# Relu attention on one core: query chunks written out, first score operands computed in place, VectorE takes the second late bank

## Chip, cores and metric

One core of a Trainium2 chip. The metric is device time in microseconds (us) of one execution, all inputs starting in HBM and the output ending there. Before the change it was measured three times: 451.36, 455.20 and 450.78 us, median 451.36 us.

## The reference

x is [2048, 128] in float32. The attention has 16 heads of width 8, and relu in place of softmax.

```python
x = L0_attn_x
h = layernorm(x)
q, k, v = split((h @ w_qkv).reshape(S, 16, 24), 3)     # 16 heads, 8 wide
w = relu(q @ k.T / sqrt(8))                            # 2048 x 2048 per head
w = w / (sum(w, -1) + 1e-6)
y = h + (w @ v) @ w_out + b_out
x = x + layernorm(y) * gamma + beta
h = layernorm(x)
real = h @ cos(theta + theta_noise)
imag = h @ sin(phi + phi_noise)
out = x + sqrt(real * real + imag * imag)
```

## The kernel before

The engines' programs are written out by hand with semaphores; nothing is scheduled by a tool. The 2048 queries are cut into four chunks of 512. A **pass** is one chunk `c`: for each of four head groups `g` (four heads each) it goes over the 16 key tiles `k` (128 keys each), so a pass has 64 **steps**, numbered `s = 16 g + k`.

A step on TensorE is `score_step` (four matmuls of 32 rows by 512 columns, one per head, the K operand with its high and low float32r parts and the Q operand with its parts side by side in 32 rows, L854) and, two steps behind (`LAG = 2`), `value_step` (the four heads' relu results times V, L884, collected in a `pv` bank over the 16 key tiles; a column of ones in V gives the sum). Scores go to three pairs of PSUM banks, `sc[0]` to `sc[2]`. Each step uses two pairs, the **early** pair (heads 0, 1) and the **late** pair (heads 2, 3). A pair is used again three pairs later, so the late half of a step waits until both relus of the early pair of the step before have been taken.

ScalarE and VectorE apply the relu and move the scores to SBUF (`w_buf`, four steps deep). ScalarE takes the first bank of the early and of the late pair (L464, L467). VectorE takes the second bank of the early pair (L602) and of the late pair (L606). At the steps in `BOTH_LATE_ACT` ScalarE takes both banks of the late pair in one activation of 1024 columns, and VectorE takes only the early one: seven, five, four and four steps of the four groups, 20 of 64 in every pass.

```python
BOTH_LATE_ACT = ((3, 8, 9, 10, 11, 13, 14), (1, 3, 8, 12, 15), (3, 7, 11, 15), (3, 7, 11, 15))
```

Beside the relus, VectorE has other work at fixed steps: `normalise` at step 3 of each group (L615 to L619), the low parts of K and Q (`low_part`, L580), in pass 0 the range reduction of the FFN angles (`trig_angles`, L630 to L646, steps 9 to 15 of group 1 and step 0 of group 2), and from pass 1 on the residual and layernorms of the chunk before (`after_pass`, L656 to L690).

Pass 0 is written out. Passes 1 to 3 are one hardware loop on each engine (`with pe.Fori(1, NC) as c`, the same on ScalarE and VectorE; SyncE and GpSimd have a shorter one), in which the semaphore values to wait for are computed in registers. The last line of the loop on TensorE is the score and value work of step 63; the next instruction after the branch is the score of step 0.

**The start.** The first 512 rows of x are loaded in one DMA (L303), normalised (`statistics`, L560 to L566; `normalise_x`, L572), transposed on TensorE (L773), copied by ScalarE (L434) and multiplied by the K and Q weights (L785, L791). ScalarE writes the high float32r part (L438, L442), VectorE the low part (L580), and then DMAs spread them over the partitions of `k_rep` and `q_rep` (row `4 r + j` holds row `r` of the high or low part), because a score matmul wants the four products high and low side by side. The first score waits for `q_lo_ready`, six dummy matmuls (`warm_up`, L809) and the DMAs. On GpSimd the three copies of the weights (L350) come when they have landed, then the padding of V for group 0 (`pad_v`, memsets L354, L355), then the normalisation of the chunks 1 to 3 (L363, L366).

Into the first ten steps of pass 0 are put the transposes and projections of the chunks 2 and 3, at hooks like `((0, 3), lambda: project_k(2))`, which stand after the score of the next step.

## Time and profile before

| what | value |
|---|---|
| median of three runs | 451.36 us |
| the profiled execution | 452.41 us |
| its span, first to last instruction | 450.6 us |
| mean granted TensorE clock in it | 0.986 |
| score starts in the span (L854) | 19.0 us to 431.5 us |
| TensorE busy | 431.3 us, 96% |
| VectorE busy | 335.6 us, 74% |
| ScalarE busy | 342.2 us, 76% |

The profiled execution took 1.8 us more than its span, and 1.05 us more than the median of the runs. In the rows, PE is TensorE's matmul and PEld its weight load, DVE is VectorE, ACT ScalarE, POOL GpSimd and SPq the DMA queue of SyncE. A timeline row has the start in us, the time in us, the engine, the line, the operation and its operands, and how many were merged; in brackets stands the idle time ahead of it with what ended it. Rows of L854 and L884 are the four score or value matmuls of one step (fp32 matmuls count as two). "issue" is time in which the engine waited for nothing that the profile shows. A step is measured from one L854 row to the next.

### The profile page before, as it was taken

To read this page: it belongs to the slowest core of one execution; us is meant where nothing else is said; L and a number is where in the kernel's file an instruction comes from. 1 tells how busy PE (TensorE), PEld (TensorE's weight loads), DVE (VectorE), ACT (ScalarE), POOL (GpSimd) and SP (SyncE) were. 2 spreads that over 40 slices of the span, in tenths; PEclk is the share of its full clock that TensorE was granted. 3 is DMA by queue.
4 is the path that set the end of the run, shared out by engine and by line. 5 is a ranking of instruction groups with operands and counts; after the bars stand their busy time and mean duration, and the time that the engine had idled before them with its cause. 6 is when DMAs were issued, how large, how long until landed. Compare 5 with 4: busy or idle time off the path is not lost.

```text
span 450.6 us, 10092 instructions
## 1 busy us (share of the span) xinstructions
PE 431.3 (96%) x3374; PEld 134.9 (30%) x3374; DVE 335.6 (74%) x685; ACT 342.2 (76%) x595; POOL 41.1 (9%) x52
## 2 busy tenths in 40 slices
PE   5899999999999999999979999999979999999995
PEld 4523222222223232222223232222213232222234
DVE  5674788777787867877757966878747976778757
ACT  1578878788788878888857878888857878888853
POOL 3794000000000001000000001000000001100001
PEclk8899999999999999999999999999989999999998
DMA  5217830000010000000000000100010000000000
GB/s 157 70 31 149 162 83 25 1 17 8 1 25 2 25 0 24 26 14 14 5 24 1 23 1 1 48 1 25 1 28 0 1 1 1 25 1 1 0 1 25
DMA packets 7021, 11.88 MB, mean 26 GB/s; under 512 B 1760, under 2 KB 3168, under 8 KB 6592
## 3 DMA queue, kind: packets, MB, share of 16 engines
q1 hardware_dynamic: 6912, 11.08, 10.1%
q8 instruction: 36, 0.59, 0.5%
q0 software_dynamic: 64, 0.13, 0.1%
q14 instruction: 9, 0.07, 0.1%
HBM read 1.77 MB, written 1.05 MB: 6 GB/s over the span
## 4 chain that ended last, share of the span: by engine, by line
PE 91%; ACT 3%; DVE 3%; issue 2%; DMA 1%; ACTq 0%; DVEq 0%
PE pv L884 55%; PE sc L854 26%; PE pv L891 3%; PE pv L932 1%; PE pv L791 1%; ACT w_buf L467 1%; DMA x_sb<-x_dram 1%; ACT w_buf L464 1%; PE pv L801 1%; PE pv L905 1%; PE sc L785 1%; PE pv L785 0%; ACT xT L434 0%; PE sc L773 0%; DVE x L690 0%
## 5 line engine op out<-in xcount | busy, mean ns | idle before, releaser
L884 PE MATMUL pv<-w_buf,v_sb 128*32 128x512 f32 x2048 | 274.3, 607 | 0.4 <-issue 0.4
L602 DVE TENSOR_SCALAR w_buf<-sc 128x512 f32<-128x512 f32 x256 | 177.0, 691 | 93.3 <-PE sc L854 82.2
L464 ACT ACTIVATE w_buf<-sc 128x512 f32<-128x512 f32 x256 | 153.2, 598 | 81.7 <-PE sc L854 80.7
L467 ACT ACTIVATE w_buf<-sc 128x512 f32<-128x512 f32 (+1 forms) x256 | 186.4, 728 | 0.0
L854 PE MATMUL sc<-q_rep,k_rep 32*128 32x512 f32 x1024 | 137.3, 495 | 7.1 <-issue 5.8
L854 PEld LDWEIGHTS sc<-q_rep,k_rep 32*128 32x128 f32 x1024 | 55.0, 182 | 222.6 <-ACT w_buf L464 169.1
L606 DVE TENSOR_SCALAR w_buf<-sc 128x512 f32<-128x512 f32 x176 | 119.8, 681 | 0.3 <-PE sc L854 0.3
L884 PEld LDWEIGHTS pv<-w_buf,v_sb 128*32 128x32 f32 x2048 | 40.8, 108 | 65.2 <-issue 31.7
L397 POOL TENSOR_TENSOR x<-x,mv 128x512 f32<-128x512 f32 (+1 forms) x5 | 4.4, 885 | 319.7 <-DVE x L690 319.7
L809 PE MATMUL pv<-ident 128*128 128x128 f32 x76 | 10.5, 302 | 1.5 <-POOL ident L345 1.5
L809 PEld LDWEIGHTS pv<-ident 128*128 128x128 f32 x76 | 10.2, 217 | 2.0 <-POOL ident L345 1.5
L476 ACT COPY pv_sb<-pv 128x512 f32<-128x512 f32 x15 | 8.8, 588 | 1.5 <-PE pv L884 1.4
L891 PE MATMUL pv<-ident,pv_sb 128*128 128x128 f32 x60 | 9.9, 287 | 0.0
L407 POOL TENSOR_TENSOR mag<-sq 128x256 f32<-128x256 f32 x6 | 4.4, 730 | 54.9 <-ACT sq L501 54.9
L891 PEld LDWEIGHTS pv<-ident,pv_sb 128*128 128x128 f32 x60 | 6.3, 141 | 3.7 <-issue 3.7
L932 PE MATMUL pv<-ffn_w,x1T 128*128 128x256 f32 x24 | 6.8, 405 | 0.0
L560 DVE BATCH_NORM_STATS2 stats<-x_sb 128x6 f32<-128x128 f32 x16 | 3.4, 278 | 4.3 <-DMA x_sb<-x_dram 4.3
L411 POOL TENSOR_TENSOR x<-x,mag 128x512 f32<-128x512 f32 x3 | 3.8, 1281 | 18.4 <-ACT mag L511 18.4
L511 ACT ACTIVATE mag<-mag,iv_p 128x128 f32<-128x128 f32 x16 | 5.5, 409 | 0.0
L354 POOL MEMSET v_sb<- 128x1472 f32 x4 | 5.3, 1336 | 0.0
L791 PE MATMUL pv<-xT,w 128*128 128x512 f32 x8 | 5.3, 749 | 0.0
L388 POOL TENSOR_TENSOR xn<-xn,bout_b 128x512 f32<-128x512 f32 x4 | 5.1, 1282 | 0.0
(100 smaller groups left out, 151.3 us busy)
## 6 DMA issues: line engine op xcount, KB each, us to landing
q_rep<-q_lo SPq DMA_DIRECT2D x32, 64.0 KB, 2.1
q_rep<-q_hi SPq DMA_DIRECT2D x30, 64.0 KB, 2.1
k_rep<-k_hi SPq DMA_DIRECT2D x6, 256.0 KB, 4.0
k_rep<-k_lo SPq DMA_DIRECT2D x6, 256.0 KB, 5.3
x_sb<-x_dram SPq DMA_DIRECT2D x4, 256.0 KB, 3.9
out_dram<-x SPq DMA_DIRECT2D x3, 256.0 KB, 2.5
k_rep<-k_hi SPq DMA_DIRECT2D x8, 64.0 KB, 2.0
k_rep<-k_lo SPq DMA_DIRECT2D x8, 64.0 KB, 2.1
```

What stands on the lines that cost most here:

```text
L464: nc.scalar.activation(w_buf[:, s % W_STEPS, 0, :], early[:, 0, :], ACT.Relu).then_inc(relu[0], 1)
L467: nc.scalar.activation(w_buf[:, s % W_STEPS, 2:2 + n, :], late[:, 0:n, :], ACT.Relu).then_inc(relu[0], 1)
L476: nc.scalar.copy(pv_sb[:, :], bank[:, :]).then_inc(pv_out, 1)
L511: last = nc.scalar.activation(mag[:, t, :], mag[:, t, :], ACT.Sqrt, scale=iv_p[:, 1, t:t + 1])
L602: nc.vector.tensor_scalar(w_buf[:, s % W_STEPS, 1, :], early[:, 1, :], 0.0, None, ALU.max).then_inc(relu[1], 2 if act_takes_both(s) else 1)
L606: nc.vector.tensor_scalar(w_buf[:, s % W_STEPS, 3, :], late[:, 1, :], 0.0, None, ALU.max).then_inc(relu[1], 1)
L791: nc.tensor.matmul(q_bank[c], w3[:, 0, :], xT[:, c * CW:(c + 1) * CW], start=True, stop=True).then_inc(q_done, 1)
L809: nc.tensor.matmul(pv[0][:, 0:P], ident[:, :], ident[:, :], start=True, stop=True)
L854: last = nc.tensor.matmul(sc[buf][:, i % 2, :], k_rep[rows, g, k * P:(k + 1) * P], q_rep[rows, g, :], start=True, stop=True)
L884: last = nc.tensor.matmul(bank[32 * i:32 * i + 32, :], v_sb[:, k, HPG * g + i, :], w_buf[:, s % W_STEPS, i, :], start=(k == 0), stop=(k == ...
L891: last = nc.tensor.transpose(bank[:, n * P:(n + 1) * P], src(t), ident[:, :])
L932: last = nc.tensor.matmul(bank[:, m * 2 * D:(m + 1) * 2 * D], x1T[:, t * P:(t + 1) * P], ffn_w[:, :, :].rearrange("p c d -> p (c d)"), sta ...
```

## The change

There are three parts.

1. **Loops.** The hardware loops over chunks become Python loops, so the passes 1 to 3 are written out on all five engines, and wait values are constants. The rotation of the bank pairs simply runs on (before, one bank was skipped at step 36 of a pass so that a pass ended where it began).
2. **The start.** `w_rep` holds the weight columns of the first four heads, each four times. Two matmuls with it (`project_rep`) give the first chunk's K and Q already spread over the 128 rows. ScalarE rounds them to float32r (`k_head`, `q_head`), and VectorE writes bank minus this head in the rows that are to hold the low part and the head itself in the others, in one instruction each (`low_rows_of`). No DMA is needed for the first four steps of group 0. The ordinary K and Q projections of chunk 0 (for the groups 1 to 3) move into the pass, with K of chunk 1. x tiles 0, 1 and 2, 3 come by two DMAs on two queues, tiles are transposed one by one, and xT is copied in halves. `pad_v(0)` goes ahead of the weight copies on GpSimd. The warm-up ahead of the first score goes.
3. **Relus.** ScalarE takes both late banks at five steps of a pass 1 to 3 (9, 10, 11, 13, 14 of group 0) and at none of pass 0. So VectorE takes 20 + 3 x 15 = 65 more late banks.

```diff
-BOTH_LATE_ACT = ((3, 8, 9, 10, 11, 13, 14), (1, 3, 8, 12, 15), (3, 7, 11, 15), (3, 7, 11, 15))
-TURN = 2 * (2 * NT + 4)
+FIRST_BOTH_LATE = ((), (), (), ())
+BOTH_LATE = ((9, 10, 11, 13, 14), (), (), ())
...
-        def pair_bank(pair):
-            return (pair if pair < TURN else pair + 1) % PSUM_PAIRS
+        def pair_bank(c, s, late):
+            return (2 * (STEPS * c + s) + late) % PSUM_PAIRS
...
-                sp.dma_start(x_sb[:, 0:TPC, :], x_v[:, 0:TPC, :]).then_inc(x_loaded[0], 16)
+                sp.dma_start(x_sb[:, 0:2, :], x_v[:, 0:2, :]).then_inc(x_loaded[0], 16)
...
-                for c in range(NC):
-                    sp.wait_ge(k_hi_ready, c + 1)
+                for c in range(1, NC):
+                    sp.wait_ge(k_hi_ready, k_turn(c))
...
+                sp.wait_ge(k_hi_ready, NC)
+                sp.wait_ge(k_lo_ready, NC)
+                sp.wait_ge(q_hi_ready, 1)
+                sp.wait_ge(q_lo_ready, 1)
                 for g in range(1, G):
                     replicate_q(0, g)
                     replicate_k(g, 0, S, k_loaded[g])
...
+                pad_v(0)
                 pool.wait_ge(wqkv_loaded, 16)
+                for n in (1, 0):
+                    src = wqkv_sb[:, :].rearrange("p (h c d) -> p c h d", h=H, c=3)[:, n, 0:HPG]
+                    nc.gpsimd.tensor_copy(w_rep[:, n, :].rearrange("p (h d j) -> p h d j", h=HPG, j=4),
+                                          src.unsqueeze(3).to_broadcast([P, HPG, HD, 4])).then_inc(w_rep_ready, 1)
...
-                pad_v(0)
                 normalise_x(1)
-                pool.wait_ge(q_hi_ready, 1)
-                for j in (0, 2):
-                    pool.dma_start(q_rep[j:P:4, 0, :].bitcast(F32), q_hi[0:32, 0:CW].bitcast(F32)).then_inc(q_first, 16)
...
+                def take_head(head, bank, n, ready):
+                    act.wait_ge(rep_done, n + 1)
+                    nc.scalar.copy(head[:, :], bank).then_inc(ready, 1)
+                act.dma_start(x_sb[:, 2:TPC, :], x_v[:, 2:TPC, :]).then_inc(x_second, 16)
                 root(0)
-                take_xT(0)
+                for half in range(2):
+                    act.wait_ge(xT_done, half + 1)
+                    cols = slice(half * 2 * P, (half + 1) * 2 * P)
+                    nc.scalar.copy(xT[:, cols], xT_bank[0][:, half, 0:2 * P]).then_inc(xT_ready, 1)
                 root(1)
-                take_k(0)
-                take_q(0)
+                take_head(k_head, sc[1][:, 0, :], 0, k_head_ready)
                 root(2)
+                take_head(q_head, pv[0][:, :], 1, q_head_ready)
+                take_v(0)
                 take_xT(1)
-                take_v(0)
-                take_k(1)
-                root(3)
...
+                def low_rows_of(out, head, bank, n, ready):
+                    dve.wait_ge(ready, 1)
+                    nc.vector.scalar_tensor_tensor(out=out, in0=head[:, :].bitcast(F32), scalar=low_rows[:, n:n + 1],
+                                                   in1=bank, op0=ALU.mult, op1=ALU.add).then_inc(rep_ready, 1)
                 statistics(0)
                 normalise_x(0)
                 statistics(1)
                 statistics(2)
-                take_k(0)
-                take_q(0)
-                statistics(3)
-                take_k(1)
+                low_rows_of(k_rep[:, 0, 0:CW], k_head, sc[1][:, 0, :], 1, k_head_ready)
+                low_rows_of(q_rep[:, 0, :], q_head, pv[0][:, :], 0, q_head_ready)
...
-                run_pass(0, [((0, 4), lambda: take_k(2)), ((0, 6), lambda: take_k(3)),
+                run_pass(0, [((0, 0), lambda: take_k(1)), ((0, 1), lambda: statistics(3)),
+                             ((0, 3), lambda: take_k(2)), ((0, 5), lambda: take_k(3)),
+                             ((0, 6), lambda: take_k(0)), ((0, 7), lambda: take_q(0)),
...
-                transpose_x(0)
+                transpose_first()
+                pe.wait_ge(xT_ready, 2)
+                project_rep(1, sc[1][:, 0, :])
+                project_rep(0, pv[0][:, :])
                 pe.wait_ge(w3_ready, 3)
-                project_k(0)
-                project_q(0)
                 project_v(0)
                 transpose_x(1)
-                project_k(1)
-                pe.wait_ge(q_lo_ready, 1)
-                warm_up(WARM_UP // 2)
...
-                run_pass(0, [((0, 1), lambda: transpose_x(3)), ((0, 3), lambda: project_k(2)),
-                             ((0, 5), lambda: project_k(3)), ((0, 7), lambda: project_v(2)),
+                run_pass(0, [((0, 0), lambda: transpose_x(2)), ((0, 1), lambda: project_v(1)),
+                             ((0, 2), lambda: project_k(2)), ((0, 3), lambda: transpose_x(3)),
+                             ((0, 4), lambda: project_k(3)), ((0, 5), lambda: project_k(0)),
+                             ((0, 6), lambda: project_q(0)), ((0, 7), lambda: project_v(2)),
                              ((0, 9), lambda: project_v(3))]
...
-                with pe.Fori(1, NC) as c:
+                for c in range(1, NC):
                     run_pass(c, after_pass(c - 1))
```

The order of TensorE's instructions at the start, before. `xn` is the normalised x, `w` the sorted weights, `sc` and `pv` PSUM banks; L854 is the first score.

```order
L773 MATMUL sc<-ident,xn 128x128 [waits xn_ready]
L773 MATMUL sc<-ident,xn 128x128 x3
L785 MATMUL sc<-xT,w 128x512 [waits xT_ready,w3_ready]
L791 MATMUL pv<-xT,w 128x512
L801 MATMUL sc<-w,xT 128x128 x4
L773 MATMUL sc<-ident,xn 128x128 [waits xn_ready]
L773 MATMUL sc<-ident,xn 128x128 x3
L785 MATMUL sc<-xT,w 128x512 [waits xT_ready]
L809 MATMUL pv<-ident 128x128 [waits q_lo_ready]
L809 MATMUL pv<-ident 128x128 x5
L854 MATMUL sc<-q_rep,k_rep 128x512 [waits k0_loaded0,xT_ready,q_loaded0,q_first]
```

The same place after the change; L899 is now the score, L808 the projection with `w_rep`.

```order
L802 MATMUL sc<-ident,xn 128x128 [waits xn_tile] x4
L808 MATMUL sc<-xT,w_rep 128x512 [waits w_rep_ready,xT_ready]
L808 MATMUL pv<-xT,w_rep 128x512 [waits w_rep_ready]
L852 MATMUL sc<-w,xT 128x128 [waits w3_ready]
L852 MATMUL sc<-w,xT 128x128 x3
L820 MATMUL pv<-ident,xn 128x128 [waits xn_ready]
L820 MATMUL pv<-ident,xn 128x128 x3
L899 MATMUL sc<-q_rep,k_rep 128x512 [waits xT_ready,rep_ready]
L899 MATMUL sc<-q_rep,k_rep 128x512
L899 MATMUL sc<-q_rep,k_rep 128x512 [waits rep_ready]
L899 MATMUL sc<-q_rep,k_rep 128x512
L831 MATMUL pv<-xT,w 128x512 [waits xT_ready]
```

The K projection of chunk 1 and the warm-up no longer stand ahead of the first score, and the first score waits for VectorE (`rep_ready`) and no longer for a DMA.

The end of TensorE's loop over the passes, before: after the last value step the branch goes back to the loop's first score.

```order
L854 MATMUL sc<-q_rep,k_rep 128x512 [waits relu_dve,relu_act]
L854 MATMUL sc<-q_rep,k_rep 128x512
L884 MATMUL pv<-w_buf,v_sb 32x512 [waits relu_dve,relu_act]
L884 MATMUL pv<-w_buf,v_sb 32x512 x3
L969 REGISTER_ALU
L969 COMPARE_AND_BRANCH
```

The turn from pass 1 to pass 2 after the change.

```order
L932 MATMUL pv<-w_buf,v_sb 32x512 [waits relu_dve,relu_act]
L932 MATMUL pv<-w_buf,v_sb 32x512 x3
L899 MATMUL sc<-q_rep,k_rep 128x512 [waits relu_dve,relu_act,q_loaded0]
L899 MATMUL sc<-q_rep,k_rep 128x512
L899 MATMUL sc<-q_rep,k_rep 128x512 [waits relu_dve,relu_act]
L899 MATMUL sc<-q_rep,k_rep 128x512
```

The branch is gone; the matmuls and their order are the same.

VectorE in pass 0, group 1, steps 12 and 13, before; `turns` and `angles` belong to the FFN angles.

```order
L602 TENSOR_SCALAR w_buf<-sc 128x512 [waits scores_act,trig_own]
L641 SCALAR_TENSOR_TENSOR angles<-turns,angles 128x256
L602 TENSOR_SCALAR w_buf<-sc 128x512 [waits scores_act,trig_own]
L606 TENSOR_SCALAR w_buf<-sc 128x512 [waits scores_dve]
L641 SCALAR_TENSOR_TENSOR angles<-turns,angles 128x256
```

After:

```order
L632 TENSOR_SCALAR w_buf<-sc 128x512 [waits scores_act,trig_own]
L636 TENSOR_SCALAR w_buf<-sc 128x512 [waits scores_dve]
L671 SCALAR_TENSOR_TENSOR angles<-turns,angles 128x256
L632 TENSOR_SCALAR w_buf<-sc 128x512 [waits scores_act,trig_own]
L636 TENSOR_SCALAR w_buf<-sc 128x512 [waits scores_dve]
L671 SCALAR_TENSOR_TENSOR angles<-turns,angles 128x256
```

The late relu of step 12 has come in between; the rest of the row of work is unchanged.

## Rows read from the trace of the kernel before

**Rows 1.** The page, busy time by engine.

```profile
PE 431.3 (96%) x3374; PEld 134.9 (30%) x3374; DVE 335.6 (74%) x685; ACT 342.2 (76%) x595; POOL 41.1 (9%) x52
```

**Rows 2.** Timeline of PE, pass 0 to pass 1 (straight into the loop).

```profile
123.58 0.54 PE L854 MATMUL sc<-q_rep,k_rep 32*128 32x512 f32 x4
...
127.91 0.51 PE L854 MATMUL sc<-q_rep,k_rep 32*128 32x512 f32 x4
```

**Rows 3.** Timeline of PE, pass 1 to pass 2 (branch taken).

```profile
223.26 0.51 PE L854 MATMUL sc<-q_rep,k_rep 32*128 32x512 f32 x4
...
227.70 0.73 PE L854 MATMUL sc<-q_rep,k_rep 32*128 32x512 f32 x4 [2.94 <-issue]
...
230.79 1.06 PE L884 MATMUL pv<-w_buf,v_sb 128*32 128x512 f32 x7 [0.39 <-issue]
231.78 0.51 PE L854 MATMUL sc<-q_rep,k_rep 32*128 32x512 f32 x4
```

**Rows 4.** Timeline of PE, pass 2 to pass 3 (branch taken).

```profile
327.14 0.51 PE L854 MATMUL sc<-q_rep,k_rep 32*128 32x512 f32 x4
...
331.47 0.72 PE L854 MATMUL sc<-q_rep,k_rep 32*128 32x512 f32 x4 [2.83 <-issue]
336.12 0.50 PE L854 MATMUL sc<-q_rep,k_rep 32*128 32x512 f32 x4
```

**Rows 5.** Windows: stretch and length, busy time PE, PEld, DVE, ACT, POOL, PEclk, DMA share, GB/s.

```profile
126.48:223.26 96.78, 96.78 (x789) 27.64 (x786) 76.54 (x149) 79.27 (x138) 3.78 (x4) 1.00 0.05 14
...
10.50:12.50 2.00, 1.95 (x3) 0.95 (x4) 1.27 (x9) 0.01 (x1) 1.83 (x2) 0.50 0.00 0
```

**Rows 6.** DMA queues, 126.48 to 223.26 us: packets, MB, share.

```profile
q8 instruction: 8, 0.13, 0.5%
```

**Rows 7.** Timeline of all engines, the start.

```profile
4.82 0.76 POOL L350 COPY w<-wqkv_sb 128x128 f32<-128x128 f32 x3 [3.32 <-DMA wqkv_sb<-w_qkv_dram]
...
5.52 1.32 POOL L354 MEMSET v_sb<- 128x1472 f32 x1
5.64 1.37 DVE L565 TENSOR_SCALAR inv_var<-mv 128x4 f32<-128x4 f32 x1
...
7.49 1.12 DVE L572 TENSOR_SCALAR xn<-x_sb,mv,rstd 128x128 f32<-128x128 f32 x4 [0.27 <-ACT rstd L430]
8.52 0.87 DVE L560 BATCH_NORM_STATS2 stats<-x_sb 128x6 f32<-128x128 f32 x4
...
9.84 0.17 DVE L565 TENSOR_SCALAR inv_var<-mv 128x4 f32<-128x4 f32 x1
...
10.14 0.84 DVE L560 BATCH_NORM_STATS2 stats<-x_sb 128x6 f32<-128x128 f32 x4
...
10.55 2.05 PE L785 MATMUL sc<-xT,w 128*128 128x512 f32 x2 [0.77 <-ACT xT L434]
...
14.96 0.69 DVE L580 TENSOR_TENSOR q_lo<-pv,q_hi 128x512 fp32r<-128x512 f32 x1 [1.01 <-ACT q_hi L442]
...
18.97 0.73 PE L854 MATMUL sc<-q_rep,k_rep 32*128 32x512 f32 x4
```

**Rows 8.** Timeline of PE, step 8 of pass 0, and a K projection.

```profile
26.42 1.12 PE L785 MATMUL pv<-xT,w 128*128 128x512 f32 x2
...
33.82 0.51 PE L854 MATMUL sc<-q_rep,k_rep 32*128 32x512 f32 x4
```

**Rows 9.** Timeline of DVE: two relus in a row; later a normalisation.

```profile
62.92 0.68 DVE L602 TENSOR_SCALAR w_buf<-sc 128x512 f32<-128x512 f32 x1
63.52 0.68 DVE L606 TENSOR_SCALAR w_buf<-sc 128x512 f32<-128x512 f32 x1
...
234.44 0.17 DVE L615 TENSOR_SCALAR den<-pv 128x16 f32<-128x16 f32 x1
...
234.93 0.29 DVE L619 TENSOR_TENSOR o_sb<-pv,den 128x128 f32<-128x128 f32 x1
```

**Rows 10.** Timeline of PE, pass 0, group 1, step 10, to group 2, step 0.

```profile
65.17 0.72 PE L854 MATMUL sc<-q_rep,k_rep 32*128 32x512 f32 x4
...
74.92 0.51 PE L854 MATMUL sc<-q_rep,k_rep 32*128 32x512 f32 x4
```

More of the change, by code:

```diff
@@ L328, in _ @@
                     next_queries(0, g)
-                with sp.Fori(1, NC - 1) as c:
+                for c in range(1, NC - 1):
                     next_queries(c, 0)
@@ L414, in _ @@
                 finish(Part(0))
-                with pool.Fori(1, NC - 1) as c:
+                for c in range(1, NC - 1):
                     pool.wait_ge(x2_ready, c)
@@ L524, in run_pass @@
                             relu_step(c, NT * g + k)
-                            if k == 1 and not (isinstance(c, int) and c == 0 and g == 0):
+                            if k == 1 and not c == g == 0:
                                 take_pv(G * c + g - 1, pv[(g + 1) % 2])
@@ L616, in normalise @@
                     own(nc.vector.reciprocal(den[:, tiles, :], den[:, tiles, :]))
-                    if g == 0 and not isinstance(c, int):
+                    if g == 0 and c:
                         dve.wait_ge(oT_done, c)
@@ L719, in run_pass @@
                             relu_step(c, NT * g + k)
-                            if k == 3 and not (isinstance(c, int) and c == 0 and g == 0):
+                            if k == 3 and not c == g == 0:
                                 normalise(G * c + g - 1, pv[(g + 1) % 2], (g - 1) % G, c=c)
@@ L730, in _ @@
                          + [((1 + n // 8, 9 + n % 8 if n < 7 else n - 7), part)
-                            for n, part in enumerate(trig_angles(own))])
+                            for n, part in enumerate(trig_angles(trig))])
                 dve.wait_ge(xb_ready, 2 * NC)
                 dve.wait_ge(consts_loaded, 64)
-                with dve.Fori(1, NC) as c:
+                for c in range(1, NC):
                     run_pass(c, after_pass(c - 1))
@@ L766, in _, with transpose_first, project_rep @@
             def _(pe):
+                def transpose_first():
+                    for t in range(TPC):
+                        pe.wait_ge(xn_tile, t + 1)
+                        last = nc.tensor.transpose(xT_bank[0][:, t // 2, t % 2 * P:(t % 2 + 1) * P], xn[:, t, :], ident[:, :])
+                        if t % 2:
+                            last.then_inc(xT_done, 1)
+                def project_rep(n, bank):
+                    pe.wait_ge(w_rep_ready, 2 - n)
+                    nc.tensor.matmul(bank, w_rep[:, n, :], xT[:, 0:CW], start=True,
+                                     stop=True).then_inc(rep_done, 1)
                 def transpose_x(c):
-                    pe.wait_ge(xn_ready, c + 1)
-                    if c == 3:
+                    pe.wait_ge(xn_ready, c)
+                    if c == 2:
                         pe.wait_ge(xT_ready, 3)
+                    elif c == 3:
+                        pe.wait_ge(k_hi_ready, k_turn(2))
+                        pe.wait_ge(k_lo_ready, k_turn(2))
                     for t in range(TPC):
@@ L837, in score_step @@
                     for half in range(2):
-                        pair = 2 * s + half
-                        buf = pair_bank(pair)
-                        user, back = freed_by(pair)
-                        if not (first and back):
-                            pe.wait_ge(relu[0], 2 * STEPS * (c - back) + user + 1)
-                            pe.wait_ge(relu[1], 2 * STEPS * (c - back) + user + 1)
+                        buf = pair_bank(c, s, half)
+                        pair = 2 * (STEPS * c + s) + half
+                        if pair >= PSUM_PAIRS:
+                            for r in relu:
+                                pe.wait_ge(r, pair - PSUM_PAIRS + 1)
                         elif buf == 0:
@@ L860, in value_step @@
                     g, k = divmod(s, NT)
-                    first = isinstance(c, int) and c == 0
+                    first = c == 0
                     bank = pv[g % 2]
+                    for r in relu:
+                        pe.wait_ge(r, 2 * (STEPS * c + s) + 2)
                     if k == 0:
@@ L877, in value_step @@
                             pe.wait_ge(sq_ready, 2 * c)
+                    if first and g == 0 and k == 0:
+                        pe.wait_ge(k_hi_ready, k_turn(1))
+                        pe.wait_ge(k_lo_ready, k_turn(1))
                     if first and g == 0 and k % TPC == 0:
-                        pe.wait_ge(v_ready, max(2, k // TPC + 1))
-                    pe.wait_ge(relu[0], 2 * STEPS * c + 2 * (s + 1))
-                    pe.wait_ge(relu[1], 2 * STEPS * c + 2 * (s + 1))
+                        pe.wait_ge(v_ready, k // TPC + 1)
                     for i in range(HPG):
@@ L968, in _ @@
                 pe.wait_ge(ffn_w_ready, 1)
-                with pe.Fori(1, NC) as c:
+                for c in range(1, NC):
                     run_pass(c, after_pass(c - 1))
```

156 lines of the change are left out of this document (85 added, 71 removed).

## Prediction

> **What bounds the kernel now.** I read the page first: TensorE is busy 431.3 of the 450.6 us of the span, VectorE and ScalarE about three quarters of it [rows 1]. So the time is TensorE's list of work plus the places where it stands still, and the question for each edit is whether it shortens the list, or fills or opens such a place. The windows say the same of pass 1: 96.78 of 96.78 us busy at a granted clock of 1.00 [rows 5].
>
> Then I went through TensorE's timeline, one score row (L854) after the other, and took the distance of neighbours. A step with nothing beside it is 1.43 to 1.44 us: from 123.58 to 127.91 us lie three steps, 4.33 us [rows 2], and nearly every step of the trace has this distance. That stretch is the turn from pass 0, written out, into the loop, and it costs nothing. The two other turns, where the branch is taken, do cost: three steps from 223.26 take 8.52 us, with 2.94 us of "issue" [rows 3], and three from 327.14 take 8.98 us, with 2.83 us [rows 4]. Against 4.30 us (three times 1.433) that is 4.2 and 4.7 us. All engines have been idle or waiting for scores then, so it is not one of them that was late. The rest of TensorE's losses are the first 19 us, before the first score [rows 7], and small waits for relus, the largest group of which lies in pass 0 while VectorE works on the FFN angles [rows 10].
>
> **Part 1, the loops.** The matmuls and their order stay the same; the branch goes. What stands in the way afterwards? A turn written out is in the trace already, from pass 0 to pass 1, without a loss [rows 2]. And the first trip through the loop body is code that TensorE sees for the first time: eight packets of the instruction queue in those 96.78 us [rows 6], in which it was never idle [rows 5]. So passes 2 and 3, written out, should run as pass 1 did. The gain is 4.2 + 4.7 = 8.9 us. The lower bound is the idle time alone, 2.94 + 2.83 = 5.8 us, if what follows the gap (a further 0.39 us of issue, slower matmuls) came from something else; more than 9 can't be had here.
>
> The Trainium skill ("Runtime: NRT & Kernel Launch", section on instruction fetch) says that fetching is purely sequential and mostly hidden, and that a taken branch to a target outside the small window must fetch it first. The trace agrees with both halves: 2.94 us at a taken branch, nothing over eight packets of straight code.
>
> **Part 2, the start.** The chain now is: inverse variance, normalise, transposes, copy, K projection, Q projection, high parts, low parts, DMA, first score at 18.97 [rows 7]. By piece:
>
> - L565 took 1.37 us (5.64 to 7.01), where the same instruction took 0.17 at 9.84. Beside it ran the memset on GpSimd, 5.52 to 6.84 [rows 7]. After the change that memset comes before the weights land, but five small copies stand in its place: three took 0.76 us from 4.82 [rows 7], five at that price end at 6.1, and if the two new ones cost twice as much, 6.6. If VectorE is held until they end, L565's successor ends at 6.15 in place of 7.01: 0.9 us won. Bounds: 1.7 (it isn't held at all, ends at 5.3) and 0.4.
> - From the start of normalising (7.49) to the first projection (10.55) are 3.06 us [rows 7]. With tiles handed over one by one (0.28 us each, 1.12 for four), the last transpose and half a copy behind them I estimate 1.9 to 2.1: 1.1 won.
> - K and Q projections: L785 took 2.05 us at 10.55 and 1.12 us at 26.42 [rows 7, 8]; the granted clock around the first was 0.50, 1.2 GHz [rows 5]. TensorE had done nothing between the dummy matmuls and the transposes. This gap becomes shorter by the two items above, so the clock may hold: 0 to 2 us.
> - The low part ends at 14.96 + 0.69 = 15.65; the first score is at 18.97. These 3.3 us of DMA go wholly, as VectorE writes the operands in place.
> - But another chain then comes late: VectorE does the statistics of chunks 1 and 2 before the operands. One such block took 10.14 - 8.52 = 1.62 us. From the start of normalising, about 6.65: 1.1 + 2 x 1.65 + 2 x 0.69 + 0.3 gives 12.7. That is the end if the clock holds; if it doesn't, TensorE's side ends later, at 18.97 - 0.9 - 1.1 - 3.3 = 13.7.
>
> So the first score comes at 12.7 to 13.7, say 13.0, which is 6.0 us earlier. This isn't the gain. Work that stood ahead of it moves behind it: K of chunk 1, K and Q of chunk 0, three projections at 1.06 us (1.12 in the row [rows 8], less the overlap with the next), 3.2 us. And the statistics of chunk 3 (1.7 us on VectorE) now lie between the relus of steps 1 and 2, when only a step or two of work is in hand, so TensorE waits. Going through the first steps, with relus at 0.60 and the inserted work in its order, I find two waits of some 0.6 us there and one of 0.5 for the V copy, which stands behind `root(3)` on ScalarE. Before, step 8 began at 33.82, 14.85 us after the first score [rows 8]; of this about 1 us was waiting. After, it should begin 14.85 + 3.2 + 0.6 = 18.7 after it, at 31.7: 2.1 to 2.2 us earlier. Bounds: 4.3 earlier (no port wait, clock held, no new waits) and 1 later (start at 14.5, waits of 5). The DMAs for groups 1 to 3 start behind `q_lo_ready`, about a step later than now; as they had some 2.5 us to spare in my reading of when they landed, I put this at nothing.
>
> The Trainium skill ("SBUF — State Buffer", on who interferes with whom) has it that GpSimd and a VectorE `tensor_scalar` of this kind lock each other out for a whole instruction. The row of 1.37 us agrees; the rule speaks against the five copies, which lie exactly where L565 and the normalisation now fall.
>
> **Part 3, the relus.** VectorE gets 65 more late banks. One costs it 0.60 us, from the start of one relu to the next (62.92 to 63.52 [rows 9]), 39 us in all, so its busy time goes to about 375 of 441 us. It isn't the bound on average: two relus are 1.20 us in a step of 1.43. What counts are the steps with other work.
> - `normalise` takes from 234.44 to 235.22, 0.78 us [rows 9]. In its step TensorE has four transposes more, 0.59 us; with the 0.23 spare of the step that is 0.82. It fits. Nothing.
> - Group 0 of passes 1 to 3 keeps its five steps; step 8, which it loses, has an output projection of 1.1 us on TensorE beside it. Nothing.
> - Step 8 of the groups 1 to 3 of pass 0 has a Q projection beside it in the same way. Nothing.
> - The FFN angles in pass 0: the six steps from 65.17 take 9.75 us [rows 10] where six free ones take 8.60, so they already lose 1.15. ScalarE's help goes at steps 12 and 15 (and 8, where there is cover): 2 x 0.60 = 1.2, up to 1.8 us more. I take 1.3.
> - Bounds of the whole part: 0, as ScalarE becomes freer (its table loads start earlier), and 4 if each normalisation leaks 0.2 us.
>
> **The sum.** 8.9 + 2.2 - 1.3 = 9.8 us less. The profiled execution took 452.41 us, so 442.6; the median of the runs is 1.05 us lower: 441.6, which I round to 441.5.
>
> **The rivals.**
> 1. *The start gives nothing.* The clock falls to 0.50 as it does now [rows 5], the first score comes at 14 to 14.5, and the steps behind it are starved by statistics and copies. Then 8.9 - 0 - 1.3 = 7.6: 443.8. For it: five copies at a bad moment, many hooks in eight steps. Against: 3.3 us of DMA that go for certain. 0.15.
> 2. *VectorE leaks at every group.* If the transposes don't give cover because `normalise` must wait for them, 15 normalisations leave VectorE 0.5 us behind each, 7.5 us, and the angles 1.8: 8.9 + 2.2 - 9.3 = 1.8, so 449.6. For it: the kernel before has ScalarE take both banks at step 3 of several groups. Against: the waits at step 4 are small even where it doesn't. 0.07.
> 3. *The turns keep their cost.* The 2.9 us belong to something else at the end of a pass than the branch. Then only 2.2 - 1.3 remain: 450.5. Against: rows 2. 0.04.
> 4. *Slower: straight code stalls.* With the passes 2 and 3 written out, every block of new instructions on TensorE makes it wait, as after the branch. The two passes bring some 16 packets [rows 6]; the 0.39 us in rows 3 for each would give back 6 us, and 2.9 us each would add 46, so 441.5 + 46 = 487. It decides from 0.6 us a packet (9.8 / 16). Against: no idle time over eight packets in pass 1 [rows 5, 6]. 0.03.
>
> **How the numbers follow.** The forecast has 0.71. Faster by over 1% (under 446.8, about what a measurement of this kernel can tell from no change) are the forecast, rival 1 and a little of rival 2: 0.88. Within 1% are the rest of rival 2 and rival 3: 0.09. Slower is rival 4: 0.03. The range: 8.9 + 4.3 - 0 = 13.2 at best gives 438.2, and rival 1 with a leak of 2 us gives 446. It leaves out rivals 2 to 4, and some of the edges.
>
> **What would show it.** In the profile after, the steps around both turns should be 1.43 us apart, without a row of "issue" near 2.9 us, and the clock 1.00 from the start on. The first score should be at 12.7 to 13.7 and step 8 at 31 to 32.5. VectorE should be busy for about 375 us, and the six steps of the angles should take 10.9 to 11.5 us. I am wrong if issue waits appear within passes 2 and 3, if steps 4 and 5 of each group grow beyond 1.5 us, or if the first eight steps take more than 20 us.

## The result, and the profile after

The changed kernel takes 440.13 us (median of 4 runs, 439.92 to 440.23) against 452.72 us for the kernel before (4 runs, 450.78 to 455.20): ratio 0.9718, 95% interval 0.9662 to 0.9774. The forecast was 441.5 us in a range of 438.2 to 446.0. The profiled span fell from 450.6 to 438.1 us, 12.5 us, where the sum had 9.8.

The page after, busy time by engine and granted clock in 40 slices (answers to [rows 1]):

```profile
PE 427.6 (98%) x3366; PEld 131.5 (30%) x3366; DVE 374.1 (85%) x755; ACT 319.7 (73%) x598; POOL 40.4 (9%) x52
...
PEclk9999999999999999999999999999999999999999
```

VectorE is at the 375 us forecast. Where TensorE's time went is seen from the starts of its score rows. The turn from pass 1 to pass 2 after, answering to [rows 3]:

```profile
220.09 0.51 PE L899 MATMUL sc<-q_rep,k_rep 32*128 32x512 f32 x4
...
221.52 0.51 PE L899 MATMUL sc<-q_rep,k_rep 32*128 32x512 f32 x4
221.96 1.06 PE L932 MATMUL pv<-w_buf,v_sb 128*32 128x512 f32 x8
...
224.39 0.51 PE L899 MATMUL sc<-q_rep,k_rep 32*128 32x512 f32 x4
```

Three steps take 4.30 us, where they took 8.52. The timeline of the start after, all engines, answering to [rows 7] and [rows 8]:

```profile
4.75 0.52 POOL L364 COPY w_rep<-wqkv_sb 128x128 f32<-128x128 f32 x2 [1.86 <-DMA wqkv_sb<-w_qkv_dram]
...
5.21 0.77 POOL L368 COPY w<-wqkv_sb 128x128 f32<-128x128 f32 x3
...
5.48 0.28 DVE L591 TENSOR_SCALAR inv_var<-mv 128x4 f32<-128x4 f32 x1
...
6.25 1.11 DVE L598 TENSOR_SCALAR xn<-x_sb,mv,rstd 128x128 f32<-128x128 f32 x4 [0.27 <-ACT rstd L439]
...
8.21 1.12 PE L808 MATMUL sc<-xT,w_rep 128*128 128x512 f32 x2 [0.46 <-ACT xT L467]
...
11.33 0.75 DVE L617 SCALAR_TENSOR_TENSOR q_rep<-q_head,low_rows,pv 128x512 fp32r<-128x512 f32 x1
...
12.13 0.51 PE L899 MATMUL sc<-q_rep,k_rep 32*128 32x512 f32 x4
...
31.11 0.51 PE L899 MATMUL sc<-q_rep,k_rep 32*128 32x512 f32 x4
```

The instruction on `inv_var` ends 1.25 us earlier than before (5.76, not 7.01): it ended while the last of the five copies was still running (until 5.98), so it was not held for all five. The projection runs at full speed (1.12 us). The first score is at 12.13, step 8 at 31.11.

All kernels can be read by the same stretches, each the distance of two score rows in its timeline. A turn is three steps, 4.30 us when nothing is lost; the two turns are those from pass 1 to 2 and from 2 to 3.

| kernel | first score | step 8 | steps 8 to 63 | one pass, steps 2 to 63 | two turns | span |
|---|---|---|---|---|---|---|
| before | 18.97 | 33.82 | 89.76 | 95.35 | 8.53, 8.98 | 450.6 |
| changed | 12.13 | 31.11 | 89.47 | 95.15 | 4.30, 4.30 | 438.1 |
| e1 loops only | 17.98 | 32.75 | 89.75 | 95.14 | 4.31, 4.30 | 440.4 |
| e2 changed, old table | 12.06 | 31.12 | 89.80 | 95.04 | 4.31, 4.31 | 438.2 |
| e3 loops and table | 17.90 | 32.73 | 89.35 | 95.15 | 4.29, 4.30 | 440.0 |
| e4 TensorE alone loops | 19.31 | 34.16 | 89.74 | 95.08 | 9.97, 8.56 | 452.2 |
| e5 only TensorE written out | 17.87 | 32.73 | 89.76 | 95.37 | 4.31, 4.30 | 440.7 |
| e6 padding put back | 13.94 | 33.01 | 89.47 | 95.19 | 4.30, 4.30 | 440.1 |
| e10 e6, longer warm-up | 13.07 | 31.93 | 89.45 | 95.12 | 4.31, 4.30 | 438.9 |
| e12 e3, padding first | 16.30 | 31.03 | 89.36 | 95.18 | 4.29, 4.30 | 438.4 |
| e9 VectorE takes all | 12.16 | 31.14 | 89.43 | 97.79 | 4.30, 4.30 | 446.1 |
| e7 angles spread | 12.04 | 31.02 | 88.56 | 95.17 | 4.30, 4.30 | 437.2 |
| e8 e7 and step 1 | 12.16 | 31.17 | 88.55 | 94.97 | 4.30, 4.30 | 436.7 |
| e11 pass 0 rearranged | 12.34 | 31.32 | 87.84 | 94.96 | 4.30, 4.29 | 436.1 |

One stretch is not in the table, from the last score row to the end of the span. It is 19.5 us in e1, e3, e4 and e12 and 19.15 in all the others. TensorE's work in it is the same; the 0.36 us more lie behind the last output, between two closing semaphore instructions of GpSimd (0.45 us apart in e1, 0.09 in the changed kernel). It comes with writing out the other engines' loops in the kernel before (e5, where they stay, hasn't it); its cause is open. Spans of these four kernels are compared with the others' with these 0.36 us in mind.

### The profile page after: what moved, and what is told of

The parts are those of the page before. It is cut to its first block, busy times and chain, and to the rows that moved or that the text cites. A ratio compares the mean times of both kernels' runs of the same rounds, so it can differ in the third digit from the quotient of the medians.

```text
span 438.1 us, 9146 instructions
## 1 busy us (share of the span) xinstructions
PE 427.6 (98%) x3366; PEld 131.5 (30%) x3366; DVE 374.1 (85%) x755; ACT 319.7 (73%) x598; POOL 40.4 (9%) x52
## 3 DMA queue, kind: packets, MB, share of 16 engines
HBM read 1.77 MB, written 1.05 MB: 6 GB/s over the span
## 4 chain that ended last, share of the span: by engine, by line
PE 93%; DVE 3%; ACT 1%; DMA 1%; POOL 0%; issue 0%; DVEq 0%
PE pv L932 58%; PE sc L899 26%; PE pv L939 3%; PE pv L980 1%; PE pv L831 1%; PE pv L840 1%; DMA x_sb<-x_dram 1%; PE pv L852 1%; PE pv L953 1%; DVE stats L586 0%; DVE x L720 0%; PE sc L939 0%; PE sc L980 0%; PE pv L820 0%; ACT L495 0%
## 5 line engine op out<-in xcount | busy, mean ns | idle before, releaser
L632 DVE TENSOR_SCALAR w_buf<-sc 128x512 f32<-128x512 f32 x256 | 176.8, 691 | 47.9 <-PE sc L899 23.6
L636 DVE TENSOR_SCALAR w_buf<-sc 128x512 f32<-128x512 f32 x241 | 164.0, 680 | 0.3 <-PE sc L899 0.3
L482 ACT ACTIVATE w_buf<-sc 128x512 f32<-128x512 f32 (+1 forms) x256 | 158.3, 618 | 0.0
L899 PE MATMUL sc<-q_rep,k_rep 32*128 32x512 f32 x1024 | 135.9, 494 | 1.2 <-DVE w_buf L632 0.6
L899 PEld LDWEIGHTS sc<-q_rep,k_rep 32*128 32x128 f32 x1024 | 53.4, 181 | 216.3 <-ACT w_buf L479 157.6
L860 PE MATMUL pv<-ident 128*128 128x128 f32 x64 | 9.4, 317 | 1.5 <-POOL ident L352 1.5
L860 PEld LDWEIGHTS pv<-ident 128*128 128x128 f32 x64 | 9.2, 232 | 1.5 <-POOL ident L352 1.5
L400 POOL TENSOR_TENSOR x_beta<-x_beta,beta_b 128x512 f32<-128x512 f32 x4 | 5.1, 1270 | 0.0
```

Of the source, the lines that this page charges most:

```text
L482: nc.scalar.activation(w_buf[:, s % W_STEPS, 2:2 + n, :], late[:, 0:n, :], ACT.Relu).then_inc(relu[0], 1)
L632: nc.vector.tensor_scalar(w_buf[:, s % W_STEPS, 1, :], early[:, 1, :], 0.0, None, ALU.max).then_inc(relu[1], 2 if both else 1)
L636: nc.vector.tensor_scalar(w_buf[:, s % W_STEPS, 3, :], late[:, 1, :], 0.0, None, ALU.max).then_inc(relu[1], 1)
L860: nc.tensor.matmul(pv[0][:, 0:P], ident[:, :], ident[:, :], start=True, stop=True)
L899: last = nc.tensor.matmul(sc[buf][:, i % 2, :], k_rep[rows, g, k * P:(k + 1) * P], q_rep[rows, g, :], start=True, stop=True)
```

## Experiments on the loops

**e1**, the kernel before with all loops written out:

```diff
-                with pe.Fori(1, NC) as c:
+                for c in range(1, NC):
                     run_pass(c, after_pass(c - 1))
```

The same on the other four engines.

> The kernel before with the loops over chunks written out on all five engines, nothing else. Theory A (the taken branch costs 4.2 and 4.7 us at the two turns): no idle time at the turns, span 450.6 - 8.9 = 441.7 us, granted clock 1.00 after the start. Rival B (the 2.9 us belong to something else at the end of a pass): the two waits stay, span near 450. Rival C (straight code stalls on fetching): issue waits spread over passes 2 and 3, span above 445.

Measured: 442.91 us (442.20 to 443.39, 4 runs), before beside it 453.18 (449.45 to 454.85, 7 runs), ratio 0.9794, interval 0.9738 to 0.9850; span 440.4. Both turns are gone, no issue wait came in. Theory A holds, B and C fall. The span is 1.3 us better than forecast: 1.1 us were gained before step 8, where nothing was edited (in this profile the clock stood at 0.50 for 3.4 us of the start, in the profile of before for 6.8), and 0.2 us in each of the three written-out passes, and 0.4 were lost at the end, as said above.

**e4 and e5**, which engine's branch it is: e4 writes out every engine but TensorE, e5 TensorE alone.

> The kernel before with the loops written out on every engine but TensorE. If TensorE's own branch is the cost (theory A), the two turns keep 2.8 to 2.9 us of issue and the span is near 450.6. If the branch of ScalarE, VectorE or SyncE was what TensorE really waited for (rival), the gap goes and the span is near 441.7.

> The kernel before with only TensorE's loop written out; SyncE, GpSimd, ScalarE and VectorE keep theirs. If the cost is TensorE's branch alone: span 441.7. Rival: each engine's branch costs it about 3 us, and those of ScalarE and VectorE now show in their turn: they are late with the relus of step 0, TensorE has some 0.7 us of room there, so 2.2 us are left at each of two turns, span near 446.

Measured: e4 454.01 us, e5 442.52 us, one run each. Timeline of TensorE in e4, at the first turn, and the window behind it (columns: stretch, length, busy time of PE, PEld, DVE, ACT, POOL, clock, DMA share, GB/s):

```profile
223.35 0.51 PE L854 MATMUL sc<-q_rep,k_rep 32*128 32x512 f32 x4
223.79 1.07 PE L884 MATMUL pv<-w_buf,v_sb 128*32 128x512 f32 x8
227.91 1.02 PE L854 MATMUL sc<-q_rep,k_rep 32*128 32x512 f32 x4 [3.06 <-issue]
228.86 1.94 PE L884 MATMUL pv<-w_buf,v_sb 128*32 128x512 f32 x8
...
233.32 0.80 PE L854 MATMUL sc<-q_rep,k_rep 32*128 32x512 f32 x4
```

```profile
227.50:234.50 7.00, 6.59 (x32) 1.73 (x36) 2.92 (x5) 3.10 (x6) 0.00 (x0) 0.52 0.07 17
```

And e5 at the same place:

```profile
222.19 0.51 PE L854 MATMUL sc<-q_rep,k_rep 32*128 32x512 f32 x4
...
226.50 0.51 PE L854 MATMUL sc<-q_rep,k_rep 32*128 32x512 f32 x4
```

TensorE's own branch is the whole cost of a turn: with it alone the gap is there (3.06 us), without it alone it isn't, and the rival of e5 (the others' branches show next) falls. The gap is only part of the price. In e4 TensorE then worked at a granted clock of 0.52, 1.2 GHz and not 2.4, and a value step took 1.94 us, so the turn cost 9.97 - 4.30 = 5.7 us. What the loops of the other engines cost is the 0.2 us a pass between e5 (95.37) and e1 (95.14), of which e1 gives 0.36 us back at the end.

What the branch makes TensorE wait for can be read from the instruction queue, from 220 to 236 us, in the kernel before, in e4 and in e5 (packets, MB, share):

```profile
q8 instruction: 4, 0.07, 1.7%
...
q8 instruction: 4, 0.07, 1.8%
...
q8 instruction: 1, 0.02, 0.5%
```

With TensorE's loop, four packets of 16 KB come in this stretch, and without it one. In the kernel before one of them starts at 224.51 us and takes 1.42 us, and the gap goes from 224.76 to 227.70; in e4 one starts at 225.20 in the gap from 224.85 to 227.91. So instructions are fetched as the gap begins. That the branch is the cause is measured. That the fetch takes the time is only a reading: the packet has ended 1.8 us before TensorE goes on, and no run changes the fetch alone.

## Experiments on the table of relus

**e2**, the changed kernel with the table of before:

```diff
-FIRST_BOTH_LATE = ((), (), (), ())
-BOTH_LATE = ((9, 10, 11, 13, 14), (), (), ())
+FIRST_BOTH_LATE = ((3, 8, 9, 10, 11, 13, 14), (1, 3, 8, 12, 15), (3, 7, 11, 15), (3, 7, 11, 15))
+BOTH_LATE = ((3, 8, 9, 10, 11, 13, 14), (1, 3, 8, 12, 15), (3, 7, 11, 15), (3, 7, 11, 15))
```

> The changed kernel with the old table (ScalarE takes both late banks at 20 of 64 steps in every pass). Theory A (VectorE has the room, and a ScalarE activation of 1024 columns frees the late pair later than two engines side by side do): slower than the change by about 0.6 us of span, 438.7, with waits at steps 12 and 15 of group 1 in pass 0 and at step 4 or so of the group with a table load. Rival B (as forecast, VectorE's 65 more banks cost 1.3 us): faster than the change, span 436.8.

Measured: 440.06 us (439.97 to 440.08), against 440.13 for the change; spans 438.2 and 438.1. Both theories miss: moving 65 banks is worth nothing. It isn't that nothing happens. Pass 0 gains 0.33 us with the new table, and the passes 1 to 3 lose 0.1 each. Within pass 0, step 3 of group 1 takes 2.02 us with the new table and 2.23 with the old one. From step 26 to step 34 the new table takes 13.10 us and the old one 12.69: the angle work indeed costs 0.4 more. From step 45 to step 54 it takes 14.72 us and the old one 15.15, as ScalarE, which no longer takes two banks at step 3 of group 3, starts its table load 0.4 us sooner after the score. In the passes 1 to 3 it is step 3 of group 1 that loses, 2.42 us against 2.21.

**e3**, e1 with the new table (the second line is for pass 0):

```diff
-BOTH_LATE_ACT = ((3, 8, 9, 10, 11, 13, 14), (1, 3, 8, 12, 15), (3, 7, 11, 15), (3, 7, 11, 15))
+BOTH_LATE_ACT = ((9, 10, 11, 13, 14), (), (), ())
+FIRST_BOTH_LATE_ACT = ((), (), (), ())
```

> The kernel before with loops written out and the new table of relus; start and bank rotation as before. Theory A: 0.6 us less than loops alone, span 441.1. Rival B: 1.3 us more than loops alone, span 443.0. What then lies between this and the changed kernel is the start: by the steps 2.7 us up to step 8, so this minus 438.1 should be about 3 us (with 0.3 for the bank that is no longer skipped).

Measured: 442.33 us (441.89 to 443.08), span 440.0, 0.4 us under e1, inside the spread of either. It says the same as e2. Step 8 is at 32.73, so the start of the change is worth 1.6 us against this profile, not 3. The bank rotation, which e3 leaves as it was, is worth nothing that shows: a pass takes 95.15 us in both kernels, and the steps 8 to 63 take 89.35 us here and 89.47 in the changed one.

**e9**, the changed kernel with the last five steps of help taken away:

```diff
-BOTH_LATE = ((9, 10, 11, 13, 14), (), (), ())
+BOTH_LATE = ((), (), (), ())
```

> The changed kernel with VectorE taking the late bank at every step (the five steps of group 0 in passes 1 to 3 go too). Theory (what a late bank costs depends on whether TensorE has other work or room beside it): in steps 9 to 14 VectorE already has about 5 us of layernorm work, no cover, and 0.23 us of room a step, so each of the 5 relus costs nearly its 0.60 us: 3 x 2 to 3 us, span 444 to 447. Rival (late banks cost nothing anywhere, as moving 65 of them did): span 438.1 to 438.6.

Measured: 447.86 us (447.76 to 448.13), span 446.1. VectorE in pass 1, group 0, steps 10 and 11, from the timeline of e9:

```profile
139.94 0.69 DVE L632 TENSOR_SCALAR w_buf<-sc 128x512 f32<-128x512 f32 x1
140.54 0.68 DVE L636 TENSOR_SCALAR w_buf<-sc 128x512 f32<-128x512 f32 x1
141.15 0.18 DVE L701 BATCH_NORM_AGGREGATE mv_p<-stats_p 128x2 f32<-128x6 f32 x1
...
141.86 0.66 DVE L632 TENSOR_SCALAR w_buf<-sc 128x512 f32<-128x512 f32 x1
142.44 0.68 DVE L636 TENSOR_SCALAR w_buf<-sc 128x512 f32<-128x512 f32 x1
143.03 1.13 DVE L710 SCALAR_TENSOR_TENSOR y<-y,mv_p,gamma_b 128x128 f32<-128x128 f32 x4
```

Every row begins before or as the last one ends: VectorE is full. A pass grows by 97.79 - 95.15 = 2.64 us, 0.53 for each of the five banks, near the whole 0.60. So fifteen late banks cost 8 us in these steps, and sixty-five cost nothing net elsewhere. The forecast's way of pricing (is there room or cover beside the bank?) is right; the rival, that late banks are free, falls.

## Experiments on the start

**e6**, the changed kernel with one piece put back:

```diff
-                pad_v(0)
                 pool.wait_ge(wqkv_loaded, 16)
...
+                pad_v(0)
                 normalise_x(1)
```

> The changed kernel with the padding of V for group 0 put back behind the weight copies on GpSimd. Theory (a VectorE tensor_scalar is held up to the end of GpSimd's instruction): the small instruction on inv_var, 0.28 us in the changed kernel, takes 1.2 to 1.5 us again, normalising starts about 1.2 us later, the first score comes at 13.3 and not at 12.1, and if the longer pause costs TensorE its clock, later still (14 or more). Span 439.3 to 441. Rival: another chain ends last at the start (the statistics of chunks 1 and 2, or GpSimd), so that the span stays at 438.1 to 438.5.

Measured: 441.62 us (440.60 to 441.89), span 440.1. From its timeline:

```profile
5.59 0.30 DVE L591 TENSOR_SCALAR inv_var<-mv 128x4 f32<-128x4 f32 x1
...
6.05 1.33 POOL L357 MEMSET v_sb<- 128x1472 f32 x1
...
6.38 1.79 DVE L598 TENSOR_SCALAR xn<-x_sb,mv,rstd 128x128 f32<-128x128 f32 x4 [0.28 <-ACT rstd L439]
...
9.01 1.70 PE L808 MATMUL sc<-xT,w_rep 128*128 128x512 f32 x2 [0.46 <-ACT xT L467]
...
10.51 1.92 PE L808 MATMUL pv<-xT,w_rep 128*128 128x512 f32 x2
...
13.94 0.51 PE L899 MATMUL sc<-q_rep,k_rep 32*128 32x512 f32 x4
```

The victim was another than expected. `inv_var` slips through in 0.30 us, since two more copies now stand ahead of the memset, and it is the normalisation that is held: 1.79 us for 1.11. TensorE now pauses 1.05 us ahead of the transposes, not 0.33; at 9.4 us the clock falls to 0.50, and the two projections take 1.70 and 1.92 us for 1.12 and 1.02. Together the first score comes 1.8 us later, and so does step 8 (1.9).

**e10** separates the two: e6 with a longer warm-up.

```diff
-WARM_UP = 12
+WARM_UP = 20
```

> The kernel with the padding put back (first score 13.94, clock fallen to 0.50 at 9.4 us) with 20 dummy matmuls at the start and not 12, so that TensorE is busy until about 7.3 us, nearly to the first transpose. Theory (of the 1.8 us, about 0.8 are the time that VectorE was held by the memset, and the rest the clock that fell in the pause it made): the clock stays at 1.00, the first score comes at 12.9 to 13.1, span near 439.1. Rival (it is all the held VectorE, or the chain over the statistics): first score stays at 13.9, span 440.1.

Measured: 440.79 us (440.71 to 441.43), span 438.9, first score at 13.07. Windows of e6, then of e10, with the columns as above:

```profile
9.50:12.50 3.00, 3.00 (x6) 1.29 (x5) 2.48 (x13) 1.04 (x4) 2.32 (x3) 0.50 0.07 21
```

```profile
6.00:9.00 3.00, 3.00 (x25) 2.87 (x24) 2.70 (x10) 0.28 (x2) 1.40 (x2) 1.00 0.73 149
9.50:12.50 3.00, 2.88 (x14) 1.92 (x15) 2.65 (x13) 1.59 (x5) 2.43 (x3) 1.00 0.14 40
```

With TensorE busy without a pause from 6 to 9 us the clock stays at 1.00. Of the 1.8 us, 0.9 were the fallen clock and 0.9 the held VectorE.

**e12** asks whether the new operands are needed for the gain: e3, that is the start of before, with `pad_v(0)` ahead of the weight copies and nothing else.

```diff
+                pad_v(0)
                 pool.wait_ge(wqkv_loaded, 16)
...
-                pad_v(0)
                 normalise_x(1)
```

> The kernel with loops written out and the new table, with the start of before (span 440.0, step 8 of pass 0 at 32.73), in which only the padding of V for group 0 moves ahead of the weight copies on GpSimd. With the new start the same move was worth 1.8 to 1.9 us (step 8 at 33.01 and 31.11). Theory (this one move is nearly the whole gain of the start, and the operands projected in place gain nothing net, since what no longer stands before the first score stands behind it): normalising starts about 1.2 us earlier, the clock holds, step 8 at 30.8 to 31.3, span 438.1 to 438.5. Rival (the old start waits for its DMAs and the dummy matmuls whatever the memset does, so the new operands are needed to have the gain): step 8 at 32 or later, span 439.3 or more.

Measured: 440.31 us (440.16 to 440.69, 6 runs), ratio to before 0.9717 (0.9679 to 0.9755), span 438.4. TensorE's timeline:

```profile
16.30 0.63 PE L856 MATMUL sc<-q_rep,k_rep 32*128 32x512 f32 x4 [1.19 <-DMA q_rep<-q_lo]
...
31.03 0.51 PE L856 MATMUL sc<-q_rep,k_rep 32*128 32x512 f32 x4
...
418.88 0.51 PE L856 MATMUL sc<-q_rep,k_rep 32*128 32x512 f32 x4
```

And the last score row of the changed kernel:

```profile
418.98 0.50 PE L899 MATMUL sc<-q_rep,k_rep 32*128 32x512 f32 x4
```

Its first score still waits for the DMA and comes 4.2 us later than in the changed kernel, but step 8 comes 0.08 us earlier, and so does the last score, by 0.10. The whole gain of the start is in the place of one memset. The operands projected in place, the second x queue and the halved copies are worth nothing that can be told from noise. The 0.2 us between the medians (440.31 against 440.13) are not theirs: they lie in the 0.36 us at the end of the span.

## A version that is faster than both

**e7** spreads the angle work over every second step and moves the two table loads.

```diff
-                         + [((1 + n // 8, 9 + n % 8 if n < 7 else n - 7), part)
+                         + [(((1, 9), (1, 11), (1, 13), (1, 15), (2, 5), (2, 10), (2, 12))[n], part)
                             for n, part in enumerate(trig_angles(trig))])
...
-                             ((3, 8), lambda: take_q(3)), ((2, 12), trig), ((3, 3), sqrt_table)])
+                             ((3, 8), lambda: take_q(3)), ((3, 7), trig), ((3, 11), sqrt_table)])
```

> The changed kernel with the parts of the angle range reduction on every second step or wider (steps 9, 11, 13, 15 of group 1, 5, 10, 12 of group 2), and the two ScalarE table loads beside TensorE's other work (sine at step 7 of group 3, before a Q projection, square root at step 11). Theory: VectorE has about 0.23 us of room in a free step and TensorE some 0.7 us of tolerance, so 0.4 to 0.6 us of extra work every second step costs nothing: the 1.65 us of waits in steps 27 to 33 go, and the 1.0 us behind the table load too, span 435.5. Rival: what VectorE is given beyond its room costs the same wherever it stands: the span stays within 0.5 us of 438.1.

Measured: 438.99 us (438.94 to 439.04), span 437.2: 0.9 us, not 2.6. The waits around the angles fell to 0.16 and 0.34 us in group 1 and twice 0.17 in group 2, but the table load at step 7 of group 3 still cost 0.9 us, three steps on: the copy of the next Q projection stands behind it on ScalarE, VectorE waits 1.57 us for that copy, and its relus are late.

**e8** adds ScalarE's help at step 1 of group 1 in passes 1 to 3.

```diff
-BOTH_LATE = ((9, 10, 11, 13, 14), (), (), ())
+BOTH_LATE = ((9, 10, 11, 13, 14), (1,), (), ())
```

> The same as the one with the angles spread, and in addition ScalarE takes both late banks at step 1 of group 1 in passes 1 to 3, where VectorE computes an inverse variance. If VectorE's backlog causes the 0.40 us wait at step 3 there: 3 x 0.2 us less, as in the kernel before (0.20). If ScalarE's copy of pv in the same step is what is late: no gain or 0.2 us more each.

Measured: 438.45 us (438.37 to 438.51), 0.5 us less; a pass goes from 95.17 to 94.97, 0.2 us each as expected. VectorE's backlog is the cause of that wait.

**e11** is e8 with the angle work placed from group 0 of pass 0 on, the two roundings as parts of their own (eight parts, not seven), and the load of the sine table apart from the sine.

```diff
-                         + [(((1, 9), (1, 11), (1, 13), (1, 15), (2, 5), (2, 10), (2, 12))[n], part)
+                         + [(((0, 10), (0, 12), (0, 14), (1, 0), (1, 6), (1, 9), (1, 12), (1, 15))[n], part)
...
+                def sine_table():
+
+                    nc.scalar.activation(spare_act[:, :], rstd[:, 0:1], ACT.Sin)
...
-                             ((3, 8), lambda: take_q(3)), ((3, 7), trig), ((3, 11), sqrt_table)])
+                             ((3, 8), lambda: take_q(3)), ((2, 3), sine_table), ((2, 6), trig), ((3, 3), sqrt_table)])
```

> The kernel with ScalarE's help at step 1 of group 1 (span 436.7), with the angle work of pass 0 cut into eight parts of at most 0.45 us and placed from step 10 of group 0 on, three steps apart where there is no cover; the sine table is loaded at step 3 of group 2, beside the transposes, by a one-element sine, and the sine itself follows at step 6. Theory (0.23 us of room a step, so 0.45 us needs two to three steps, and 1.5 us on ScalarE beside 0.59 us of transposes costs 0.2 us as the square root's table does): waits of pass 0 after step 16 fall from about 1.9 to 0.4 us, span 435.2. Rival (the waits move with the work): 436.3 or more.

Measured: 437.62 us (437.60 to 437.92), ratio to before 0.9654 (0.9617 to 0.9691), span 436.1: 2.5 us under the changed kernel, and 0.6 us of span under e8, where 1.5 were expected. ScalarE's timeline at the table load:

```profile
76.34 1.28 ACT L499 ACT_TABLE_LOAD   x1
77.64 0.20 ACT L499 ACTIVATE spare_act<-rstd 128x1 f32<-128x1 f32 x1
77.74 0.58 ACT L479 ACTIVATE w_buf<-sc 128x512 f32<-128x512 f32 x1
```

Beside the transposes of step 3 it costs TensorE 0.21 us where it cost 1.0. The last four angle parts still cost 0.16 to 0.18 us each, though they stand three steps apart, and the two table loads 0.2 us each, so about 1.1 us of waits are left after step 16, where 0.4 were expected.

## Why the prediction was right, and where it was off

**The loops** were right in mechanism and size: two turns of 4.2 and 4.7 us gone (e1), by TensorE's branch alone (e4, e5). Rivals 3 and 4 fall: the turns don't keep their cost, and no straight stretch shows an issue wait. The section on instruction fetch in the Trainium skill's "Runtime: NRT & Kernel Launch" agrees, for TensorE: a packet of instructions comes as each gap begins, though it fills only about the first 1 us of the 2.9. For the four other engines a taken branch showed no cost at the turn (e5). The sum left out that the written-out programs of the others give 0.2 us a pass.

**The start**: the pieces were forecast as 0.9 for the memset, 1.1 for handing over tile by tile, 0 to 2 for the clock, 3.3 for the DMA. The first score (12.7 to 13.7 forecast) came at 12.13 and step 8 (31.7) at 31.11. From the start of normalising to the first projection it is now 1.96 us (6.25 to 8.21), where 1.9 to 2.1 were said. But e12, which hands over as before, needs 2.59 us there and not 3.06, with the clock at 1.00: tile by tile is worth 0.6, and the other 0.5 of the 1.1 belong to the clock, which stood at 0.50 from 8 us on before. The step that failed is the reason: "These 3.3 us of DMA go wholly". They do, and three projections come in their place behind the first score, and waits with them. The sum gave the new data path 0.6 us net (1.1 + 3.3 - 3.2 - 0.6); by step 8 it gave nothing (e12). What gave the gain is the memset, 0.9 us of held VectorE and 0.9 of clock (e6, e10). The clock had only a range of 0 to 2 us in the prediction. That the total of the start came near is in part luck. I took from the locking rule of the Trainium skill's page "SBUF — State Buffer" a warning against the five copies; the trace shows that VectorE comes in between two short copies (0.28 us), while one long memset holds it for its whole length.

**The relus**: forecast 1.3 us slower, measured 0.0 (e2: medians 440.06 and 440.13). The term was mis-sized on both sides. The six steps of the angles, which were to take 10.9 to 11.5 us, take 10.01 in the changed kernel:

```profile
62.24 0.68 PE L899 MATMUL sc<-q_rep,k_rep 32*128 32x512 f32 x4
...
72.25 0.73 PE L899 MATMUL sc<-q_rep,k_rep 32*128 32x512 f32 x4
```

So this sign missed. They took 9.75 before. Over the whole stretch, steps 26 to 34, the new table costs 0.4 us, not 1.3, though VectorE has three banks more there, 1.8 us. My reading is that ScalarE, taking two banks, had itself freed the late pair later; no run isolates that. And "its table loads start earlier" was left as a bound at 0 when it was worth 0.4. "4 if each normalisation leaks 0.2 us" did not happen, only the one of group 1 leaks 0.2 us in the passes 1 to 3, and rival 2 falls.

**The sum**: 12.5 us of span against 9.8. By the stretches of the table it is 2.71 to step 8, 0.29 from there to the end of pass 0, 0.20 in each of three passes and 4.23 and 4.68 at the turns, 12.51 together. The sum had 2.2, -1.3, nothing and 8.9: the missing 2.7 are 0.5 at the start, 1.6 in pass 0, where the angles cost nothing net, and 0.6 in the passes, which e1 shows too, with the old relus. The kernel before is itself uncertain by more than that: its runs beside the experiments go from 449.45 to 455.64.

That the forecast of the time is only 1.4 us off while the sum is 2.7 off is luck. The forecast took away 1.05 us because the median before lay under the profiled execution; after the change the median lies 0.2 us over it (440.13 against 439.92), and this hides half of the error. One bound of the start is also wrong as arithmetic: a first score at 14.5 us with 5 us of waits puts step 8 at 14.5 + 14.85 + 3.2 + 4 = 36.6 us, 2.7 us later than before and not 1. Nothing came near it.

Two things stated ahead of the prediction are wrong. The angle parts of the kernel before stand at steps 9 to 15 of group 1 only, none at step 0 of group 2; seven parts end there, and the wait runs on. And the rows 10 are one step off in their title: they go from step 11 of group 1 to step 1 of group 2.

## What to carry to other kernels

Moving work from ahead of the first useful instruction to behind it is no gain by itself: measure a start by a milestone at which both versions have done the same work, here step 8, not by the first score. The place of one 1.3 us memset on GpSimd, next to a VectorE instruction on the critical chain, was worth more than a new data path, and the pause that it caused on TensorE counted twice, through the clock. Price a shift of work between two engines by place: 0.53 us a bank where the receiver is full, nothing net where it has room.

## What the runs showed of the hardware

- The spread of the kernel before is a matter of TensorE's clock. Of its runs beside the experiments, the two with a mean granted clock of 0.996 took 449.45 and 449.96 us, and the eight with 0.976 took 454.74 to 455.64; the others lie between. With the same loop on TensorE a turn cost 4.2 us where the clock stayed at 1.00 behind the pause (before, first turn) and 4.7 and 5.7 where it fell to 1.2 GHz (before, second turn; e4, first turn). Without these pauses the changed kernel had 0.998 to 1.000 in each of its four runs, and they lie within 0.3 us. The change made the kernel not only faster but more repeatable.
- In e6 one run of four kept 0.999 and took 440.60 us, the three others had 0.995 and took 441.57 to 441.89, 1.0 to 1.3 us more. Eight more dummy matmuls (e10) brought the median down by 0.8 us.
